# Transposing the first stage's tiles in pairs, and moving one evacuation of the second stage from ScalarE to VectorE

## The chip, the cores and the metric

The kernel runs on the 8 NeuronCores of one Trainium2 chip. Each core has a tensor engine (TensorE, PE in the profile), a vector engine (VectorE, DVE), a scalar engine (ScalarE, ACT), GpSimd (POOL) and SyncE (SP), and 16 DMA engines. Every core works on one batch element, alone: the cores exchange nothing. The metric is the device time of the slowest core in microseconds (us). TensorE's clock has two levels here, 2.4 GHz (a granted clock of 1.00 in the profile) and 1.2 GHz (0.50).

## The reference

Each core computes, for its 4096 tokens of width 1024, one layer with a linear "attention" and a feed-forward part. Cut to what is computed:

```python
qkv = einsum('btd,de->bte', layernorm(x), Wqkv) + bqkv      # 1024 -> 3072
q = q / norm(q); k = k / norm(k)
kv = sum(k * v, axis=tokens)                                 # one row of 1024
x = x + einsum('btd,de->bte', q * kv, Wout) + bout
h = layer_norm(x) @ ternary_quant(w1).T + b1                 # 1024 -> 4096
h = layer_norm(gelu(h))
out = x + h @ ternary_quant(w2).T + b2                       # 4096 -> 1024
```

`kv` is a sum over all tokens, so everything after it needs a first pass over all of them. The ternary quantization needs the mean of the absolute values of a whole weight matrix before its first element can be rounded.

## The kernel before, in words

The 4096 tokens are 32 tiles of 128. The program is written by hand for each engine: every engine has its own list of instructions, in order, and semaphores say what one waits for of another. Nothing is scheduled automatically, so an instruction that waits holds up all that stand behind it on its engine.

**Stage A (to 870 us)** makes q, k and v. For tile j, SyncE loads x into `xbufA` (L293), VectorE and ScalarE compute the layer norm, ScalarE writes the normalised tile `h1buf` to a scratch in HBM (L359), and SyncE reads it back transposed into `h1T` (`h1t_tile`, L273 to L286), with eight DMA transposes of 128 rows by 128 columns, one for each 128-column block. `h1T` holds two groups of four tiles. TensorE multiplies it by Wqkv (L591): six blocks e0 to e5 of 512 columns, eight products each, into a ring of four PSUM buffers `pqkv`. VectorE takes them out three tiles later than it normalises (`dvA_back(j - 3)`, L835), and ScalarE and VectorE make `qhat`, `khat` and the sum of k times v. Beside this runs the weight quantization: GpSimd loads 128 slabs of w1 and w2 into a ring of five buffers `wstg` (L545) and writes the quantized ones back (L534, L538); VectorE sums absolute values (L785) or adds two sign tiles (L793), ScalarE makes the signs (L420, L422). One round of stage A's loop over j is called an iteration here.

Then the quantized weights are read back transposed (`w1p`, `w2p`: L309, L315) and scaled (to about 1060 us).

**Stage B (from about 1060 us)** handles the tiles in 16 pairs p, j0 = 2p and j1 = 2p + 1. In a pair TensorE does, in this order: the output projection of tile j0 + 2 (`attn_mm`, L670); y1, the first feed-forward product, for both tiles (L731, 32 steps m of eight products, into two PSUM buffers that ScalarE empties with Gelu into `h4buf`, L496); the projection of tile j1 + 2; the transposition of tile j0 + 2's normalised `z1buf` as two rounds of four 128 by 128 products with the identity into the one PSUM buffer `pzT` (`zT_round`, L711), where round 1 waits until round 0 has been taken out (semaphore `bze`); then y2 of tile j0 and y2 of tile j1 (`y2_tile`). Each of the 32 steps of y2 is two products of 512 columns (L690), a one-column product that sums h (L696), and one that sums its square (L699). The squares come from VectorE (`dv_h4sq`, L1004) over a ring of four small tiles `h4sq`: TensorE's L699 of step m waits for square m, and VectorE's square m + 4 waits for that L699. After y2 of each tile VectorE computes statistics and the output (`dv_tail`, L1014 to L1054), then the front of a later tile (`dv_front`, L961 to L990); y2 of the next tile waits for `outbuf` (L1054), and its first L699 for the square behind that front. The last two rounds of `zT_round`, for tile j1 + 2, lie inside and behind y2 of j1.

The transposed tile goes from `pzT` to `z1T` in two halves of four casts: by ScalarE for tile j0 + 2 (`zT_evac_sc`, L443 to L451, called at L501), by VectorE for tile j1 + 2 (`zT_evac`, L1057 to L1065, called at L1082).

Of the kernel before, what the change touches and what calls it, by code (L numbers as in the profile page):

```python
# [11 lines left out]
AF = mybir.ActivationFunctionType  # L12
# [43 lines left out]
def build_program(T):  # L56
    NT = T // 128
    NG = NT // 4
# [17 lines left out]
    h1_d = nc.dram_tensor("h1scr", [T, D], BF16, kind="Internal").ap()  # L76
# [42 lines left out]
    ax = DSem(nc, es, "ax"); asq = S("asq"); avar = S("avar"); asd = S("asd")  # L119
    astat = S("astat"); ah1 = S("ah1")  # L120
    ah1w = DSem(nc, es, "ah1w"); ah1t = DSem(nc, es, "ah1t", nslots=4)
# [71 lines left out]
    z1T = sbB("z1T", [128, 2048], BF16, is_transpose_dest=True)  # L193
# [18 lines left out]
    pzT = psB.enter_context(nc.psum_tensor("pzT", [128, 512], F32))  # L212
# [56 lines left out]
    with es, esB, psB, nc.Block() as block:  # L269

        @block.sync
        def _(sy):
            def h1t_tile(jt):  # L273
                gt = jt // 4
                st = jt % 4
                sy.wait_ge(ah1w.h(jt % 2), 16 * (jt // 2 + 1))
                if jt >= 4:
                    sy.wait_ge(ah1t.h(jt % 4), 128 * (jt // 4))
                if gt >= 2 and st == 0:
                    sy.wait_ge(aqkv.h, 24 * (gt - 1))  # L280
                for c in range(8):
                    ah1t.inc(sy.dma_start(
                        out=h1T[:, (gt % 2) * 4096 + c * 512 + st * 128:
                                (gt % 2) * 4096 + c * 512 + (st + 1) * 128],
                        in_=h1_d[jt * 128:(jt + 1) * 128, c * 128:(c + 1) * 128],
                        transpose=True), jt)  # L286

            for g in range(NG):
                for s in range(4):
                    j = 4 * g + s  # L290
                    if j >= 2:
                        sy.wait_ge(ah1.h, j - 1)
                    ax.inc(sy.dma_start(  # L293
                        out=xbufA[:, (j % 2) * D:(j % 2 + 1) * D],
                        in_=x_d[j * 128:(j + 1) * 128, :]), j)
                    if j - 2 >= 0:
                        h1t_tile(j - 2)
            for jt in (4 * NG - 2, 4 * NG - 1):
                h1t_tile(jt)
            sy.wait_ge(ax.h(0), ax.totals()[0])  # L300
            sy.wait_ge(ax.h(1), ax.totals()[1])
            for sl in range(4):
                sy.wait_ge(ah1t.h(sl), ah1t.totals()[sl])
            bar.inc(sy.nop())
            sy.wait_ge(bar.h, 5)
            for sl in range(4):
                sy.wait_ge(dvw.h(sl), 16 * 8)
            for c in range(8):
                w1t.inc(sy.dma_start(out=w1p[:, c * H:(c + 1) * H],  # L309
                                     in_=wq1_d[:, c * 128:(c + 1) * 128],  # L310
                                     transpose=True), 16)
            for sl in range(4):
                sy.wait_ge(dvw.h(sl), 16 * 16)
            for r in range(32):
                w2t.inc(sy.dma_start(out=w2p[:, r * D:(r + 1) * D],  # L315
                                     in_=wq2_d[:, r * 128:(r + 1) * 128],
                                     transpose=True), 16)
            for j in range(NT):
                if j >= 1:
                    sy.wait_ge(batt.h, 2 * j)  # L320
                for c in range(8):
                    bqt.inc(sy.dma_start(
                        out=qT[:, c * 128:(c + 1) * 128],
                        in_=qh_d[j * 128:(j + 1) * 128, c * 128:(c + 1) * 128],
                        transpose=True), 16)
                if j >= 2:
                    sy.wait_ge(bsqx.h, j - 1)
                bx.inc(sy.dma_start(out=xbufB[:, (j % 2) * D:(j % 2 + 1) * D],
                                    in_=x_d[j * 128:(j + 1) * 128, :]), j)
            sy.wait_ge(bow.h, 16 * NT)  # L330

        @block.scalar
        def _(sc):
# [106 lines left out]
            sc.wait_ge(bar.h, 5)  # L440
            smld.inc(sc.dma_start(out=b2rowB, in_=b2_d), 16)

            def zT_evac_sc(t, r):  # L443
                g = 2 * t + r
                sc.wait_ge(bzt.h, g + 1)
                for cc in range(4):
                    c = 4 * r + cc
                    cp = sc.activation(
                        out=z1T[:, c * 256 + (t % 2) * 128:c * 256 + (t % 2) * 128 + 128],
                        in_=pzT[:, cc * 128:(cc + 1) * 128], func=AF.Copy)  # L450
                bze.inc(cp)  # L451

            def sc_front(t):
                P = (t % 2) * 16
                xr = xring[:, (t % 3) * D:(t % 3 + 1) * D]
# [32 lines left out]
            for p in range(NT // 2):  # L488
                j0, j1 = 2 * p, 2 * p + 1
                if j0 + 2 < NT:  # L490
                    sc_front(j0 + 2)
                if p >= 1:
                    sc.wait_ge(bsq4.h, 32 * j0)
                for m in range(32):
                    sc.wait_ge(by1.h, 32 * p + m + 1)
                    bh4.inc(sc.activation(  # L496
                        out=h4buf[:, m * 256:(m + 1) * 256],
                        in_=py1[m % 2][:, :], func=AF.Gelu,
                        bias=beta1c[:, m:m + 1]))
                if j0 + 2 < NT:  # L500
                    zT_evac_sc(j0 + 2, 0)  # L501
                    zT_evac_sc(j0 + 2, 1)
                sc_tail(j0)
                if j1 + 2 < NT:
                    sc_front(j1 + 2)
                sc_tail(j1)
# [61 lines left out]
        def _(te):  # L568
# [13 lines left out]
            te.wait_ge(wqkvs.h, 128)  # L582
            for g in range(NG):
                for s in range(4):
                    te.wait_ge(ah1t.h(s), 128 * (g + 1))
                    for e in range(6):
                        i = (4 * g + s) * 6 + e
                        if i >= 4:
                            te.wait_ge(aevac.h, i - 3)
                        for c in range(8):  # L590
                            mm = te.matmul(  # L591
                                out=pq[i % 4][:, :],
                                lhsT=h1T[:, (g % 2) * 4096 + c * 512 + s * 128:
                                         (g % 2) * 4096 + c * 512 + (s + 1) * 128],
                                rhs=wqkvp[:, c * E3 + e * 512:c * E3 + (e + 1) * 512],
                                start=(c == 0), stop=(c == 7))
                        aqkv.inc(mm)
                    if (g, s) == p_mtot1:
                        te.wait_ge(mpre.h, 1)
                        mtot.inc(te.matmul(out=pone[:, 0:1],  # L600
                                           lhsT=stA[:, 30:31], rhs=onesf[:, :],
                                           start=True, stop=True))
                    if (g, s) == p_mbc1:
                        te.wait_ge(mval.h, 1)
                        mbc.inc(te.matmul(out=pmb[:, 0:1], lhsT=onesrow[:, :],
                                          rhs=mrow[0:1, 0:1],
                                          start=True, stop=True))
                    if (g, s) == p_mtot2:
                        te.wait_ge(mpre.h, 2)
                        mtot.inc(te.matmul(out=pone[:, 1:2],  # L610
                                           lhsT=stA[:, 31:32], rhs=onesf[:, :],
                                           start=True, stop=True))
                    if (g, s) == p_mbc2:
                        te.wait_ge(mval.h, 2)
                        mbc.inc(te.matmul(out=pmb[:, 1:2], lhsT=onesrow[:, :],
                                          rhs=mrow[0:1, 1:2],
                                          start=True, stop=True))
# [103 lines left out]
            for p in range(NT // 2):  # L721
                j0, j1 = 2 * p, 2 * p + 1
# [4 lines left out]
                for m in range(32):  # L727
                    if 32 * p + m >= 2:
                        te.wait_ge(bh4.h, 32 * p + m - 1)
                    for c in range(8):  # L730
                        mm = te.matmul(  # L731
                            out=py1[m % 2][:, :],
# [15 lines left out]
        def _(dv):  # L748
# [323 lines left out]
            for p in range(NT // 2):  # L1072
                j0, j1 = 2 * p, 2 * p + 1
                if j0 + 2 < NT:
                    dv_front(j0 + 2)
                dv_h4sq(j0)
                dv_tail(j0)
                if j1 + 2 < NT:
                    dv_front(j1 + 2)
                dv_h4sq(j1)  # L1080
                if j1 + 2 < NT:
                    zT_evac(j1 + 2, 0)  # L1082
                    zT_evac(j1 + 2, 1)
                dv_tail(j1)
# [17 lines left out]
        "bfin": NT, "bow": 16 * NT,  # L1102
        "bzt": 2 * NT, "bze": 2 * NT,
    }
    dexpect = {"ax": 16 * NT, "ah1w": 16 * NT, "ah1t": 512 * NG,
               "aqw": 16 * NT, "wld": 16 * NLOADS,
               "dvw": 16 * (NW1 + NW2),
               "bx": 16 * NT}
# [43 lines left out]
```

## Time and profile before

| what | value |
|---|---|
| three runs | 2606.44, 2609.64, 2615.18 us; median 2609.64 |
| the profiled execution | 2606.68 us, its slowest core's span 2605.1 us |
| spans of the eight cores | 2581.4 to 2605.1 us |
| mean granted TensorE clock | 0.814 to 0.824 |
| busy: PE, DVE, ACT, POOL | 62%, 38%, 31%, 5% of the span |
| chain of work that ended last, by engine | PE 49%, DVE 12%, issue 9%, ACT 9%, DVEq 8%, DMA 7% |
| the same by line, the largest | y2 L690 19%, y1 L731 18%, qkv L591 7%, wstg loads 5% |
| landing time of an h1T transpose (SP, 256 of them) | 2.8 us |

The page cuts the span into 40 slices of 65 us. Stage A is slices 2 to 14; from slice 17 on PE's row repeats 867 867 867, which are the pairs of stage B. The page's shares are averages over both stages, so what follows is read from the trace in the stretch where each edit acts. Busy times and rows below are of the slowest core, core 0.

### The profile page before, as it was taken

How to read it: one execution, taken by the hardware profiler on the slowest of the kernel's cores; microseconds unless marked ns; L12 is line 12 of the kernel's file. 1: busy time of each engine (PE TensorE's matmuls, PEld its weight loads, DVE VectorE, ACT ScalarE, POOL GpSimd, SP SyncE). 2: the span in 40 equal slices, each digit the busy share in tenths (PEclk: the TensorE clock that was granted, in tenths of full speed). 3: DMA queues.
4: the chain of work that ended last, by engine and by line, in shares of the span. 5: the costliest groups of instructions: out<-in, count | busy, mean ns of one | idle time of the engine just before them, and what ended most of it. 6: DMA issues, size and time to landing. Idle time of an engine off the chain costs nothing.

```text
span 2605.1 us, 35302 instructions; the slowest of 8 cores (2581.4 to 2605.1 us)
## 1 busy us (share of the span) xinstructions
PE 1624.3 (62%) x10800; PEld 911.5 (35%) x10928; DVE 989.7 (38%) x2582; ACT 795.0 (31%) x1433; POOL 118.5 (5%) x217
## 2 busy tenths in 40 slices
PE   0354565453457226767867867867867867867867
PEld 0121222121123112435535535535535534534544
DVE  0456644443445223252252252252252252252243
ACT  0132356656664100313313313313313312312311
POOL 2111101111110000000000000000000000000000
PEclk9976777677778657878888888888888888888889
DMA  9776544555542590110010010010010010010000
GB/s 146 177 212 200 162 122 145 174 168 161 176 150 69 117 152 14 34 41 21 21 41 22 21 42 21 22 41 22 22 40 21 22 40 22 23 40 21 21 17 17
DMA packets 203594, 195.39 MB, mean 75 GB/s; under 512 B 160404, under 2 KB 160405, under 8 KB 203415
## 3 DMA queue, kind: packets, MB, share of 16 engines
q0 software_dynamic: 31200, 92.34, 12.9%
q1 hardware_dynamic: 157952, 67.18, 11.1%
q10 hardware_dynamic: 14264, 33.62, 3.6%
q8 instruction: 97, 1.59, 0.3%
q14 instruction: 81, 0.66, 0.1%
HBM read 117.55 MB, written 50.33 MB: 64 GB/s over the span
## 4 chain that ended last, share of the span: by engine, by line
PE 49%; DVE 12%; issue 9%; ACT 9%; DVEq 8%; DMA 7%; SPq 4%; POOL 1%; ACTq 1%; another core or an unknown queue 0%; POOLq 0%
PE py L690 19%; PE py L731 18%; PE pqkv L591 7%; DMA wstg<-w 5%; PE patt L670 3%; DVEq L962 2%; DVEq L805 2%; SPq L315 2%; SPq L309 2%; DVE outbuf L1046 2%; DVEq L1053 1%; DVE kvtmp L846 1%; DVE xring L967 1%; ACT qhat L379 1%; ACT khat L388 1%
## 5 line engine op out<-in xcount | busy, mean ns | idle before, releaser
L591 PE MATMUL pqkv<-wqkvp,h1T 128*128 128x512 bf16 x1505 | 402.3, 432 | 366.8 <-DVE qkvb L835 334.2
L690 PE MATMUL py<-w2p,h4buf 128*128 128x512 bf16 x1968 | 528.6, 398 | 134.5 <-DVE outbuf L1054 123.1
L731 PE MATMUL py<-z1T,w1p 128*128 128x256 bf16 x4096 | 491.3, 285 | 167.3 <-ACT h4buf L496 165.5
L1004 DVE TENSOR_TENSOR h4sq<-h4buf 128x128 bf16<-128x128 bf16 x1024 | 227.3, 225 | 847.9 <-PE psumSQ L699 711.1
L731 PEld LDWEIGHTS py<-z1T,w1p 128*128 128x128 bf16 x4096 | 388.9, 101 | 270.4 <-issue 172.5
L591 PEld LDWEIGHTS pqkv<-wqkvp,h1T 128*128 128x128 bf16 x1536 | 163.7, 108 | 604.9 <-issue 470.7
L496 ACT ACTIVATE h4buf<-py,beta1c 128x256 bf16<-128x256 f32 x512 | 241.1, 474 | 239.4 <-PE py L731 238.7
L699 PE MATMUL psumSQ<-onesb,h4sq 128*128 128x1 bf16 x1024 | 167.4, 163 | 76.3 <-DVE h4sq L1004 76.3
L699 PEld LDWEIGHTS psumSQ<-onesb,h4sq 128*128 128x128 bf16 x1024 | 102.7, 100 | 215.5 <-issue 104.7
L696 PE MATMUL psumSQ<-onesb,h4buf 128*128 128x1 bf16 x1024 | 173.3, 169 | 0.0
L690 PEld LDWEIGHTS py<-w2p,h4buf 128*128 128x128 bf16 x2048 | 125.5, 96 | 127.7 <-issue 127.3
L835 DVE TENSOR_TENSOR qkvb<-pqkv,bqkvb 128x512 f32<-128x512 f32 x192 | 123.7, 686 | 110.5 <-PE pqkv L591 103.6
L696 PEld LDWEIGHTS psumSQ<-onesb,h4buf 128*128 128x128 bf16 x1024 | 103.3, 101 | 138.5 <-issue 28.3
L458 ACT ACTIVATE xbufB<-xring 128x512 f32<-128x512 f32 x32 | 20.1, 629 | 402.7 <-DVE xring L967 402.7
L670 PE MATMUL patt<-woutp,qT 128*128 128x512 bf16 x495 | 118.1, 393 | 14.5 <-DMA qT<-qhscr 13.2
L480 ACT ACTIVATE stB<-stB 128x1 f32<-128x1 f32 x32 | 6.5, 203 | 308.9 <-DVE stB L1031 308.7
L480 ACT ACT_TABLE_LOAD x16 | 20.5, 1283 | 257.7 <-DVE stB L1031 257.7
L785 DVE TENSOR_REDUCE wpart<-wstg 128x1 f32<-128x1024 f32 x64 | 74.4, 1213 | 17.9 <-DMA wstg<-w 17.9
L349 ACT ACTIVATE stA<-stA 128x1 f32<-128x1 f32 x32 | 6.5, 203 | 243.7 <-DVE stA L816 243.7
L545 POOL DMA_DIRECT2D wstg<-w x128 | 68.0, 532 | 234.2 <-DVE wpart L785 233.4
L846 DVE TENSOR_TENSOR kvtmp<-khat,qkvb 128x1024 f32<-128x1024 f32 x32 | 39.2, 1226 | 98.9 <-ACT khat L388 98.9
L670 PEld LDWEIGHTS patt<-woutp,qT 128*128 128x128 bf16 x512 | 50.8, 101 | 73.3 <-issue 23.8
(126 smaller groups left out, 1275.6 us busy)
## 6 DMA issues: line engine op xcount, KB each, us to landing
wstg<-w POOLq DMA_DIRECT2D x128, 512.0 KB, 5.9
xbufA<-x SPq DMA_DIRECT2D x32, 512.0 KB, 5.0
xbufB<-x SPq DMA_DIRECT2D x32, 512.0 KB, 3.5
out<-outbuf ACTq DMA_DIRECT2D x32, 512.0 KB, 2.7
h1scr<-h1buf ACTq DMA_DIRECT2D x32, 256.0 KB, 5.1
qhscr<-qhat ACTq DMA_DIRECT2D x32, 256.0 KB, 2.4
wqkvp<-wqkv POOLq DMA_DIRECT2D x8, 768.0 KB, 28.8
h1T<-h1scr SPq DMA_TRANSPOSE x256, 2.8
```

Of the source, the lines that this page charges most:

```text
L496: bh4.inc(sc.activation(out=h4buf[:, m * 256:(m + 1) * 256], in_=py1[m % 2][:, :], func=AF.Gelu, bias=beta1c[:, m:m + 1]))
L545: wld.inc(gp.dma_start(out=wslot(i), in_=w_src(kind, ch)), i)
L591: mm = te.matmul(out=pq[i % 4][:, :], lhsT=h1T[:, (g % 2) * 4096 + c * 512 + s * 128: (g % 2) * 4096 + c * 512 + (s + 1) * 128], rhs=wqkvp ...
L670: mm = te.matmul(out=patt[:, hh * 512:(hh + 1) * 512], lhsT=qT[:, c * 128:(c + 1) * 128], rhs=woutp[:, c * D + hh * 512:c * D + (hh + 1) * ...
L690: mm = te.matmul(out=py2[:, hh * 512:(hh + 1) * 512], lhsT=h4m, rhs=w2p[:, m * D + hh * 512:m * D + (hh + 1) * 512], start=(m == 0), stop= ...
L696: te.matmul(out=psumSQ[:, m:m + 1], lhsT=h4m, rhs=onesb[:, :], start=True, stop=True)
L699: bsq4.inc(te.matmul(out=psumSQ[:, 32 + m:33 + m], lhsT=h4sq[:, (m % 4) * 128:(m % 4 + 1) * 128], rhs=onesb[:, :], start=True, stop=True))
L731: mm = te.matmul(out=py1[m % 2][:, :], lhsT=w1p[:, c * H + m * 128:c * H + (m + 1) * 128], rhs=z1T[:, c * 256:(c + 1) * 256], start=(c == ...
L785: dcons.inc(dv.tensor_reduce(out=wpart[:, col:col + 1], in_=wslot(i), axis=AX.X, op=ALU.add, apply_absolute_value=True))
L835: aevac.inc(dv.tensor_tensor(out=qkvb[:, e * 512:(e + 1) * 512], in0=pq[i % 4][:, :], in1=bqkvb[:, e * 512:(e + 1) * 512], op=ALU.add))
L846: dv.tensor_tensor(out=kvtmp[:, :], in0=khat[:, :], in1=qkvb[:, 2 * D:3 * D], op=ALU.mult)
L1004: bsq.inc(dv.tensor_tensor(out=h4sq[:, (m % 4) * 128:(m % 4 + 1) * 128], in0=h4m, in1=h4m, op=ALU.mult))
```

## The change: pairs of tiles in stage A, one evacuation in stage B

Two edits that do not touch each other.

In stage A `h1t_tile` becomes `h1t_half`: it transposes two tiles in one go, so each of its eight DMA transposes reads 256 rows and writes 256 columns of `h1T`. It is called once for every two tiles, after the x load of tile jt + 3, and waits until both tiles have been written to HBM. The semaphores `ah1t` count pairs.

In stage B `zT_evac_sc` is gone; VectorE calls `zT_evac(j0 + 2, 0)` and `zT_evac(j0 + 2, 1)` between the front of tile j0 + 2 and the squares of tile j0.

```diff
--- before.py
+++ after.py
@@ -270,20 +270,22 @@
 
         @block.sync
         def _(sy):
-            def h1t_tile(jt):
+            def h1t_half(jt):
                 gt = jt // 4
                 st = jt % 4
-                sy.wait_ge(ah1w.h(jt % 2), 16 * (jt // 2 + 1))
-                if jt >= 4:
-                    sy.wait_ge(ah1t.h(jt % 4), 128 * (jt // 4))
+                hg = jt // 2
+                sy.wait_ge(ah1w.h(0), 16 * (jt // 2 + 1))
+                sy.wait_ge(ah1w.h(1), 16 * (jt // 2 + 1))
+                if hg >= 4:
+                    sy.wait_ge(ah1t.h(hg % 4), 128 * (hg // 4))
                 if gt >= 2 and st == 0:
                     sy.wait_ge(aqkv.h, 24 * (gt - 1))
                 for c in range(8):
                     ah1t.inc(sy.dma_start(
                         out=h1T[:, (gt % 2) * 4096 + c * 512 + st * 128:
-                                (gt % 2) * 4096 + c * 512 + (st + 1) * 128],
-                        in_=h1_d[jt * 128:(jt + 1) * 128, c * 128:(c + 1) * 128],
-                        transpose=True), jt)
+                                (gt % 2) * 4096 + c * 512 + (st + 2) * 128],
+                        in_=h1_d[jt * 128:(jt + 2) * 128, c * 128:(c + 1) * 128],
+                        transpose=True), hg)
 
             for g in range(NG):
                 for s in range(4):
@@ -293,10 +295,9 @@
                     ax.inc(sy.dma_start(
                         out=xbufA[:, (j % 2) * D:(j % 2 + 1) * D],
                         in_=x_d[j * 128:(j + 1) * 128, :]), j)
-                    if j - 2 >= 0:
-                        h1t_tile(j - 2)
-            for jt in (4 * NG - 2, 4 * NG - 1):
-                h1t_tile(jt)
+                    if j >= 3 and j % 2 == 1:
+                        h1t_half(j - 3)
+            h1t_half(4 * NG - 2)
             sy.wait_ge(ax.h(0), ax.totals()[0])
             sy.wait_ge(ax.h(1), ax.totals()[1])
             for sl in range(4):
@@ -440,16 +441,6 @@
             sc.wait_ge(bar.h, 5)
             smld.inc(sc.dma_start(out=b2rowB, in_=b2_d), 16)
 
-            def zT_evac_sc(t, r):
-                g = 2 * t + r
-                sc.wait_ge(bzt.h, g + 1)
-                for cc in range(4):
-                    c = 4 * r + cc
-                    cp = sc.activation(
-                        out=z1T[:, c * 256 + (t % 2) * 128:c * 256 + (t % 2) * 128 + 128],
-                        in_=pzT[:, cc * 128:(cc + 1) * 128], func=AF.Copy)
-                bze.inc(cp)
-
             def sc_front(t):
                 P = (t % 2) * 16
                 xr = xring[:, (t % 3) * D:(t % 3 + 1) * D]
@@ -497,9 +488,6 @@
                         out=h4buf[:, m * 256:(m + 1) * 256],
                         in_=py1[m % 2][:, :], func=AF.Gelu,
                         bias=beta1c[:, m:m + 1]))
-                if j0 + 2 < NT:
-                    zT_evac_sc(j0 + 2, 0)
-                    zT_evac_sc(j0 + 2, 1)
                 sc_tail(j0)
                 if j1 + 2 < NT:
                     sc_front(j1 + 2)
@@ -582,7 +570,8 @@
             te.wait_ge(wqkvs.h, 128)
             for g in range(NG):
                 for s in range(4):
-                    te.wait_ge(ah1t.h(s), 128 * (g + 1))
+                    hg = 2 * g + s // 2
+                    te.wait_ge(ah1t.h(hg % 4), 128 * (hg // 4 + 1))
                     for e in range(6):
                         i = (4 * g + s) * 6 + e
                         if i >= 4:
@@ -1073,6 +1062,8 @@
                 j0, j1 = 2 * p, 2 * p + 1
                 if j0 + 2 < NT:
                     dv_front(j0 + 2)
+                    zT_evac(j0 + 2, 0)
+                    zT_evac(j0 + 2, 1)
                 dv_h4sq(j0)
                 dv_tail(j0)
                 if j1 + 2 < NT:
@@ -1102,7 +1093,7 @@
         "bfin": NT, "bow": 16 * NT,
         "bzt": 2 * NT, "bze": 2 * NT,
     }
-    dexpect = {"ax": 16 * NT, "ah1w": 16 * NT, "ah1t": 512 * NG,
+    dexpect = {"ax": 16 * NT, "ah1w": 16 * NT, "ah1t": 64 * NT,
                "aqw": 16 * NT, "wld": 16 * NLOADS,
                "dvw": 16 * (NW1 + NW2),
                "bx": 16 * NT}
```

VectorE in the first pair of stage B. Before, the squares of j0 (`h4sq`) follow the front's last statistic directly; `bzt` is TensorE's transposition being done, `bh4` ScalarE's Gelu, `bsq4` TensorE's L699:

```order
L988 RECIPROCAL stB<-stB 128x1 [waits bsd]
L990 TENSOR_TENSOR stB<-stB 128x1
L1004 TENSOR_TENSOR h4sq<-h4buf 128x128 [waits bh4] x4
L1004 TENSOR_TENSOR h4sq<-h4buf 128x128 [waits bh4,bsq4] x28
L1014 TENSOR_REDUCE stB<-psumSQ 128x1 [waits bsq4]
```

The same place now:

```order
L977 RECIPROCAL stB<-stB 128x1 [waits bsd]
L979 TENSOR_TENSOR stB<-stB 128x1
L1051 CAST z1T<-pzT 128x128 [waits bzt]
L1051 CAST z1T<-pzT 128x128 x3
L1051 CAST z1T<-pzT 128x128 [waits bzt]
L1051 CAST z1T<-pzT 128x128 x3
L993 TENSOR_TENSOR h4sq<-h4buf 128x128 [waits bh4] x4
L993 TENSOR_TENSOR h4sq<-h4buf 128x128 [waits bh4,bsq4] x28
L1003 TENSOR_REDUCE stB<-psumSQ 128x1 [waits bsq4]
```

All 32 squares of tile j0 now stand behind eight casts that wait for TensorE's transposition; before, the first four waited for Gelu alone.

SyncE in stage A, from its first x loads on. `ah1` is ScalarE's normalised tile, `ah1w0` and `ah1w1` its write to HBM for even and odd tiles. Before:

```order
L293 DMA xbufA<-x 128x1024 x2
L293 DMA xbufA<-x 128x1024 [waits ah1]
L282 DMA_TRANSPOSE h1T<-h1scr 128x128 [waits ah1w0]
L282 DMA_TRANSPOSE h1T<-h1scr 128x128 x7
L293 DMA xbufA<-x 128x1024 [waits ah1]
L282 DMA_TRANSPOSE h1T<-h1scr 128x128 [waits ah1w1]
L282 DMA_TRANSPOSE h1T<-h1scr 128x128 x7
```

And now:

```order
L295 DMA xbufA<-x 128x1024 x2
L295 DMA xbufA<-x 128x1024 [waits ah1] x2
L284 DMA_TRANSPOSE h1T<-h1scr 128x256 [waits ah1w0,ah1w1]
L284 DMA_TRANSPOSE h1T<-h1scr 128x256 x7
L295 DMA xbufA<-x 128x1024 [waits ah1] x2
L284 DMA_TRANSPOSE h1T<-h1scr 128x256 [waits ah1w0,ah1w1]
L284 DMA_TRANSPOSE h1T<-h1scr 128x256 x7
```

Two x loads now stand ahead of each batch of eight transposes, and the batch waits for the write of the later tile of its pair.

## Rows read from the trace of the kernel before

**Rows 1.** Waits in 1300 to 2605 us: total us, times, longest us.

```profile
PE py L731 <- ACT h4buf L496: 136.8, 13, 11.2
...
PE py L690 <- DVE outbuf L1054: 107.5, 14, 7.7
```

**Rows 2.** Timeline of PE, stage A: start, length, instruction, [idle before, releaser].

```profile
119.47 9.70 PE L591 MATMUL pqkv<-wqkvp,h1T 128*128 128x512 bf16 x32 [30.03 <-DMA h1T<-h1scr]
...
495.07 6.18 PE L591 MATMUL pqkv<-wqkvp,h1T 128*128 128x512 bf16 x16 [14.21 <-DVE qkvb L835]
...
834.05 10.52 PE L591 MATMUL pqkv<-wqkvp,h1T 128*128 128x512 bf16 x47 [0.37 <-DVE qkvb L835]
```

**Rows 3.** The chain that ended last, stage A: start, length, what.

```profile
139.63 4.32 PE pqkv L591 x14
...
509.49 4.16 DMA wstg<-w
...
591.42 5.68 DMA wstg<-w
```

**Rows 4.** Timeline of SyncE's queue.

```profile
99.61 12.01 SPq L282 DMA_TRANSPOSE h1T<-h1scr  x8
...
114.08 11.20 SPq L282 DMA_TRANSPOSE h1T<-h1scr  x8
...
473.91 10.03 SPq L282 DMA_TRANSPOSE h1T<-h1scr  x8
...
500.12 10.04 SPq L282 DMA_TRANSPOSE h1T<-h1scr  x8
...
578.78 10.02 SPq L282 DMA_TRANSPOSE h1T<-h1scr  x8
...
796.80 40.00 SPq L282 DMA_TRANSPOSE h1T<-h1scr  x24
...
915.92 53.81 SPq L315 DMA_TRANSPOSE w2p<-wq2scr  x32
```

**Rows 5.** Timeline of DVE in stage A, first tile taken out.

```profile
137.99 2.48 DVE L835 TENSOR_TENSOR qkvb<-pqkv,bqkvb 128x512 f32<-128x512 f32 x4
```

**Rows 6.** Timeline of PE around the transposition in one pair.

```profile
1398.16 0.39 PE L711 MATMUL pzT<-identb,z1buf 128*128 128x128 bf16 x4
1399.85 0.38 PE L711 MATMUL pzT<-identb,z1buf 128*128 128x128 bf16 x4 [1.31 <-ACT z1T L448]
...
1400.75 0.16 PE L699 MATMUL psumSQ<-onesb,h4sq 128*128 128x1 bf16 x1
...
1429.59 0.16 PE L699 MATMUL psumSQ<-onesb,h4sq 128*128 128x1 bf16 x1 [5.04 <-DVE h4sq L1004]
```

**Rows 7.** Timeline of ACT at the same place.

```profile
1400.33 0.79 ACT L448 ACTIVATE z1T<-pzT 128x128 bf16<-128x128 f32 x4 [0.62 <-PE pzT L711]
```

**Rows 8.** Timeline of DVE in the same pair.

```profile
1370.69 0.23 DVE L1004 TENSOR_TENSOR h4sq<-h4buf 128x128 bf16<-128x128 bf16 x1 [1.48 <-ACT h4buf L496]
...
1429.22 0.93 DVE L1004 TENSOR_TENSOR h4sq<-h4buf 128x128 bf16<-128x128 bf16 x5
...
1448.10 0.88 DVE L1062 CAST z1T<-pzT 128x128 bf16<-128x128 f32 x4 [1.27 <-PE pzT L711]
1448.90 0.18 DVE L1014 TENSOR_REDUCE stB<-psumSQ 128x1 f32<-128x32 f32 x1
```

**Rows 9.** Windows: length, busy us of PE, PEld, DVE, ACT, POOL, PEclk, DMA share, GB/s.

```profile
1333.10:1339.10 6.00, 5.66 (x36) 2.66 (x37) 2.34 (x12) 0.93 (x1) 0.00 (x0) 0.71 0.00 0
1429.59:1435.59 6.00, 5.66 (x26) 2.39 (x28) 1.87 (x10) 0.94 (x1) 0.00 (x0) 0.50 0.00 1
1366.37:1372.37 6.00, 6.00 (x36) 4.53 (x37) 0.90 (x4) 1.80 (x5) 0.00 (x0) 0.64 0.12 49
1464.02:1470.02 6.00, 6.00 (x30) 4.21 (x31) 0.90 (x4) 1.65 (x4) 0.00 (x0) 0.53 0.13 51
...
1269.37:2436.74 1167.37, 860.83 (x6649) 536.25 (x6722) 415.74 (x1344) 309.09 (x697) 0.00 (x0) 0.86 0.09 28
```

## The prediction, made before the changed kernel had run

> **What bounds the kernel now.** I read the cores' spans, the chain that ended last, and then for each edit the waits and the timelines of the stretch in which it acts. In stage B the chain runs through TensorE, so what counts is where TensorE stands still. The waits and the timeline show three such places in a pair [rows 1]: before y1's third step for ScalarE's first Gelu (about 10.8 us, behind the output and the front of a tile), before y2 of j1 for `outbuf` (7.7 us), and a little later for j1's first square. None of them is touched. A fourth, small, wait lies between the two transposition rounds. After it TensorE goes straight into y2 of j0, because four squares were made long before.
>
> In stage A TensorE is not the bound: it waits 14.2 us for VectorE [rows 2] in an iteration of some 26 us. The chain there goes round through VectorE, TensorE's last 16 products of a tile, ScalarE, VectorE, GpSimd and one weight load of 4.2 to 5.7 us [rows 3]. SyncE's transposes are not in it; they take 10 of the 26.2 us from one batch to the next [rows 4].
>
> **Edit 1: transposes in pairs.** The same bytes move in 128 DMAs instead of 256.
>
> *Cost on SyncE.* Eight transposes of 128 rows are issued in 10.03 us, 1.25 us each; the weight transposes of 1024 rows in 53.81 / 32 = 1.68 us each [rows 4]. Between these, 256 rows should take 1.25 + (0.43 / 896) x 128 = 1.31 us, so a pair's batch takes 10.5 us. Bounds: 10.0 (price by the instruction) and 20.1 us (price by the row). Per two iterations SyncE is busy 10.5 us instead of 20; it was idle over half of the time, so that frees nothing.
>
> *The middle of stage A.* The pair's batch starts when the later tile's write has landed, 5.05 us after TensorE has resumed in that iteration (495.07 and 500.12 [rows 2, 4]), and with the 2.8 us that the profile's table gives for a landing it is there after 5.05 + 10.5 + 2.8 = 18.4 us. TensorE wants the earlier tile one iteration later, behind the last 16 products of the tile before (6.18 us [rows 2]): 26.2 + 6.2 = 32.4 us. Slack 14 us; with the high bound of the batch still 4 us. The two tiles of a group reuse a half of `h1T` that was free long before. Taken: nothing. What hides it is VectorE's hold on TensorE.
>
> The Trainium skill, "DMA: Bandwidth & Descriptors", section "Anatomy of one DMA", gives each DMA a constant part of about 2 us, mostly completion. If that were on the path, 128 DMAs fewer would be worth an estimated 256 us, and the sum would be near 2380 us. The trace speaks against applying it: the issues follow each other 1.25 us apart, so these parts overlap, and nobody waits for them after the first tile. The sum goes by the rows.
>
> *The start.* TensorE's first tile waits for the first batch. Now this batch waits for tile 1 too, so it starts where tile 1's batch started, 114.08, and is issued by 125.3 [rows 4]. The first batch before (99.61 + 12.01 = 111.62 [rows 4]) was followed by TensorE at 119.47 [rows 2], 7.9 us later, which gives 133.2 us; with the usual landing of 2.8 us it is 128.1. TensorE's first 32 products take 9.70 us, so they end between 137.8 and 142.9. VectorE has them out by 137.99 + 2.48 = 140.5 now [rows 5]; TensorE's last 16 overlap that, since they may start when the first buffer is free (4.32 us for 14 from 139.63 [rows 3]). Delay 0 to 4 us; taken 2, the middle.
>
> *The end.* The last 24 transposes end at 796.80 + 40.00 = 836.80 [rows 4], so tile 31's batch began at 826.8. Tile 30 now goes with it: 826.8 + 10.5 + 2.8 = 840.1. TensorE reached tile 30 at 834.05 + 16 x 0.224 (10.52 us for 47 products) = 837.6 [rows 2]. Late by 2.5 us on a stretch where TensorE follows VectorE with 0.4 us of idle; taken 2, ends 0 and 12 (a batch of 20 us).
>
> Edit 1 together: +4 us; from -5 (transposes absent from every second iteration give the weight loads a little room) to +16.
>
> **Edit 2: the casts of tile j0 + 2 on VectorE.** There are 15 pairs with it. ScalarE loses eight casts, 1.58 us; behind them it only waits for VectorE's statistic at the end of y2 of j0, so nothing is gained there.
>
> *Round 0.* Four casts take 0.79 us on ScalarE [rows 7] and 0.88 us on VectorE [rows 8]; TensorE's round 1 waits for them: +0.09 us.
>
> *Round 1.* Now nobody waits for ScalarE's casts, and y2 follows. The squares m = 0 to 3 were done at 1370.9 [rows 8], thirty microseconds ahead, so the first L699 ran at 1400.75 [rows 6]. Afterwards VectorE waits from the end of its front until round 0. Queued behind the casts are all squares of j0, and behind these the output and the next front; TensorE waits for the first square. Round 1 ends at 1400.23, casts start at 1400.33 [rows 6, 7], take 0.88 us, and the next VectorE instruction starts 0.08 us before their nominal end, as 1448.90 after 1448.10 + 0.88 shows [rows 8]: 1401.13. From a first square's start to TensorE's L699 takes 1429.59 - 1429.22 = 0.37 us [rows 6, 8]: 1401.50. That is 0.75 us later than 1400.75. Squares then come every 0.18 us (five in 0.93) against TensorE's step of 0.48, so no second wait. Sum 0.84 us a pair, 15 x 0.84 = 12.6 us. Bounds: 0.6 us (if the square is seen at once) and 1.1 us (each semaphore wait of the new chain adding about 0.1).
>
> *What the clock makes of it.* After both long waits of a pair the clock is at 1.2 GHz when work resumes, and stays there for some microseconds. In windows of 6 us from the resumption it is 0.71 and 0.50 of full after the first wait, in one pair and the next, 0.64 and 0.53 after the second [rows 9]. The part at 1.2 GHz is thus 3.5 or 6.0 us and 4.3 or 5.7 us, and half of it is lost work: 3.9 us in the short kind of pair, 5.8 us in the long kind. The two kinds alternate along the whole stage, and twelve pairs take 1167.37 us, 97.28 each. So the pairs run in step with the clock's changes, two by two, with a mean loss of 4.85 us. Each pair longer by 0.84 us breaks this step. In the short kind the clock rose barely after 3.5 us of resumed work; if work resumes 0.8 us later against that rise, the rise falls to the later occasion, as in the long kind. I expect nearly all pairs to be of the long kind: loss 5.7 instead of 4.85, +0.86 us. A pair then takes 97.28 + 0.84 + 0.86 = 98.98 us. Bounds: all short, -0.96; all long, +0.96. I take a value near the upper end, since a delay can only move the resumption away from the early rise. 15 x 1.70 = 25.5 us.
>
> **The sum.** 25.5 + 4 = 29.5 us on the profiled execution's 2606.68: 2636 us. Its span was 2605.1, the rest is start and end. The median of the three runs is 3 us above it; the same would hold for the changed kernel: 2639 us.
>
> **The rivals.**
>
> *A, only the added wait counts.* The alternation stays as it is, by chance of the new phase, and a pair costs 0.84 us: 12.6 + 4 = 16.6, so 2626 us. For it: the added wait is the only thing in the listing. Against it: the exact alternation shows that the pair's length and the clock hang together.
>
> *B, the other side: the weight loads get faster.* In iterations without transposes the load on stage A's chain could take 4.16 us, the shortest of its late ones, instead of 5.68. If that held for all 26 iterations from tile 4 to 29, it would give 26 x 1.52 = 40 us, and the time would be 2599 us, faster. It decides from a saving of 1.1 us an iteration on. For it: halved DMAs and 10 us of idle queue. Against it: the load at 591.42, behind transposes that had all been issued by 588.8, still took 5.68 us, and the one of 4.16 us began before its transposes (500.1 to 510.2) were over [rows 3, 4]. So the length does not follow the transposes.
>
> *C, the clock falls at the transposition.* TensorE would be idle 1.4 us and again 0.8 us with half a microsecond of work between, where now it is idle once and the clock stays at 1.00. If it fell there, y2 would run its first steps at 1.2 GHz and lose what the resumption after the first wait loses in the long kind, 3.0 us: 15 x 3.0 = 45 more, 2684 us. The Trainium skill, "TensorE: Matmul & The Clock Gate", section "A second HAM failure mode: psum-queue depth-cycling", says that short idle spells between groups of matmuls can be enough to make the clock swing. By that rule the time would be this rival's. The trace does not bear it out so far: the idle 1.31 us here leaves the clock up [rows 6], and y2's steps run on at 0.48 us.
>
> **How the numbers follow.** Forecast 0.62, A 0.22, B 0.06, C 0.04, and 0.06 for a mixture of B with A, in which both edits cancel. The likeliest gives 2639 us. Its own range is 2628 to 2650 (the rhythm between 0.4 and 0.96 a pair, edit 1 between -2 and +12). The range downwards takes in A with edit 1 at -5 (2617). Upwards it takes the high ends of the wait (+4) and of edit 1: 2653. A change within 0.3% (8 us) can't be told from none. Slower by more: forecast, most of A, and C, 0.88; faster, B, 0.06; same 0.06.
>
> **What would show it.** Right: in each of 15 pairs an idle stretch of 0.7 to 0.8 us before the first L699 of j0, put down to VectorE's square; VectorE's casts there at 0.88 us, ScalarE without casts; y2 of j0 still at 0.48 us a step; pairs of 98.9 to 99.1 us on average with a mean clock in stage B no higher than 0.86; 128 transposes in stage A, eight in 10 to 11 us. TensorE's first product at 128 to 133 us. Wrong: pairs that still average under 98.3 us (rival A), iterations of stage A clearly shorter than 26 us (B), a clock of 0.50 in the stretch after round 1 (C), or TensorE waiting for `h1T` in the middle of stage A, which would mean that a batch takes far longer than 11 us.

## The result, and the profile after

The changed kernel is slower: the median of ten runs is 2642.6 us against 2608.8 us of ten runs of the kernel before, a ratio of 1.0125, 95% interval 1.0111 to 1.0139. The forecast was 2639 us. Some executions fall into a slower state of the chip, so every ratio here is of the undisturbed runs alone, while the medians are of all runs.

The profiled execution took 2641.46 us with a span of 2639.9 us on core 0, the core whose rows stood before. First stage A, PE's timeline after:

```profile
142.55 19.18 PE L580 MATMUL pqkv<-wqkvp,h1T 128*128 128x512 bf16 x79 [52.64 <-DMA h1T<-h1scr]
...
840.01 11.52 PE L580 MATMUL pqkv<-wqkvp,h1T 128*128 128x512 bf16 x47 [3.57 <-DVE qkvb L824]
851.89 10.52 PE L580 MATMUL pqkv<-wqkvp,h1T 128*128 128x512 bf16 x47 [0.36 <-DVE qkvb L824]
```

TensorE gets its first tile 23.1 us later than in [rows 2] (142.55 against 119.47; 128 to 133 had been forecast), and that is the only wait for `h1T` in the whole run: at the end of stage A its idle times are put down to VectorE, as before. VectorE, which takes the first tile out:

```profile
133.91 0.16 DVE L812 TENSOR_TENSOR stA<-stA 128x1 f32<-128x1 f32 x1
146.23 0.69 DVE L824 TENSOR_TENSOR qkvb<-pqkv,bqkvb 128x512 f32<-128x512 f32 x1 [12.16 <-PE pqkv L580]
```

It is ready 4 us earlier than in [rows 5] and then stands for 12.2 us; the first buffer goes out 8.2 us later than before. The batches of transposes, SyncE's queue:

```profile
115.82 13.24 SPq L284 DMA_TRANSPOSE h1T<-h1scr  x8
...
488.37 10.13 SPq L284 DMA_TRANSPOSE h1T<-h1scr  x8
```

Eight transposes of 256 rows are issued in 10.1 us, as fast as eight of 128 rows [rows 4]. The first batch took 13.2 us and landed 13.5 us after its last issue (115.82 + 13.24 = 129.06, TensorE at 142.55), where the first batch before landed after 7.9 us. In these 13.5 us the core's DMA engines are busy all the time (a mean share of 1.01), while beside the batch at 488.37 their share is 0.44:

```profile
129.10:142.50 13.40, 0.00 (x0) 0.00 (x0) 3.25 (x9) 1.44 (x2) 1.06 (x2) 1.00 1.01 232
488.30:502.00 13.70, 6.65 (x31) 2.83 (x29) 5.16 (x8) 9.09 (x8) 3.21 (x6) 0.84 0.44 128
```

The first batch before met full DMA engines too (shares 1.05 and 0.98), with half the bytes. That the load makes the landing so long fits, but no run varies it alone.

Now stage B, in one pair. PE and then DVE around the transposition:

```profile
1412.56 0.39 PE L700 MATMUL pzT<-identb,z1buf 128*128 128x128 bf16 x4
1414.08 0.38 PE L700 MATMUL pzT<-identb,z1buf 128*128 128x128 bf16 x4 [1.14 <-DVE z1T L1051]
1414.53 0.59 PE L679 MATMUL py<-w2p,h4buf 128*128 128x512 bf16 x2
1414.95 0.17 PE L685 MATMUL psumSQ<-onesb,h4buf 128*128 128x1 bf16 x1
1415.74 0.16 PE L688 MATMUL psumSQ<-onesb,h4sq 128*128 128x1 bf16 x1 [0.62 <-DVE h4sq L993]
```

```profile
1414.57 0.89 DVE L1051 CAST z1T<-pzT 128x128 bf16<-128x128 f32 x4 [0.64 <-PE pzT L700]
1415.37 0.86 DVE L993 TENSOR_TENSOR h4sq<-h4buf 128x128 bf16<-128x128 bf16 x5
```

The chain casts, first square, first L699 (L688 now) is there as foretold. From y2's first product to that L699 it takes 1.21 us where it took 0.46 (1400.29 to 1400.75, [rows 6] for the latter): 0.75 us more, 0.73 on the mean of the 15 pairs. From round 0 to round 1 it is 1.52 us in all pairs after and 1.41 in 14 of 15 before, 0.09 us more on the mean; only the pair of [rows 6] had 1.69. Together the two waits add 0.82 us a pair. The clock's windows after, one pair and the next after the first long wait (y2 of j1 for its first square), one pair and the next after the second (y1 for the Gelu), then the beginning of y2 of j0, and twelve pairs:

```profile
1347.30:1353.30 6.00, 5.66 (x34) 2.68 (x36) 2.21 (x12) 0.93 (x1) 0.00 (x0) 0.69 0.00 1
1446.65:1452.65 6.00, 5.66 (x37) 2.70 (x39) 2.35 (x12) 0.93 (x1) 0.00 (x0) 0.72 0.00 0
1380.70:1386.70 6.00, 6.00 (x36) 4.38 (x37) 0.00 (x0) 1.72 (x5) 0.00 (x0) 0.63 0.16 63
1480.15:1486.15 6.00, 6.00 (x38) 4.47 (x39) 0.00 (x0) 1.95 (x5) 0.00 (x0) 0.67 0.08 33
1415.90:1419.30 3.40, 3.40 (x14) 1.29 (x15) 0.99 (x5) 0.00 (x0) 0.00 (x0) 0.50 0.13 28
1281.65:2469.59 1187.94, 872.86 (x6649) 538.26 (x6722) 432.55 (x1440) 289.80 (x601) 0.00 (x0) 0.86 0.09 28
```

A pair takes 1187.94 / 12 = 99.00 us, 1.71 more than in [rows 9]; 98.98 had been forecast. But it comes about in another way. Nearly all pairs are now of the short kind after both long waits. Measured from where work resumes to where the granted clock rises, on the mean of these twelve pairs of core 0, the low stretch after the first wait was 4.65 us before and is 3.85 now, the one after the second was 4.89 and is 4.49. In exchange the clock is at 1.2 GHz for 3.4 us at the start of y2 of j0, where it was 1.00 before:

```profile
1398.50:1401.90 3.40, 2.03 (x18) 1.09 (x18) 0.45 (x2) 1.57 (x8) 0.00 (x0) 1.00 0.10 22
```

It falls so in 12 of the 15 pairs on core 0, and in 12 or 13 on every core. In the other three pairs of core 0 the clock stays up, with a second idle spell of 0.47, 0.47 and 0.83 us where the twelve have 0.53 to 0.62; the low stretches after the long waits that follow are then longer.

### The profile page after: what moved, and what is told of

The parts are those of the page before. It is cut to its first block, busy times and chain, and to the rows that moved or that the text cites. A ratio compares the mean times of both kernels' runs of the same rounds, so it can differ in the third digit from the quotient of the medians.

```text
span 2639.9 us, 35158 instructions; the slowest of 8 cores (2610.9 to 2639.9 us)
## 1 busy us (share of the span) xinstructions
PE 1629.5 (62%) x10800; PEld 911.8 (35%) x10928; DVE 1010.8 (38%) x2702; ACT 771.0 (29%) x1313; POOL 118.0 (4%) x217
## 4 chain that ended last, share of the span: by engine, by line
PE 49%; DVE 13%; issue 9%; ACT 8%; DVEq 7%; DMA 7%; SPq 5%; POOL 1%; ACTq 1%; another core or an unknown queue 0%; POOLq 0%
PE py L679 19%; PE py L720 17%; PE pqkv L580 7%; DMA wstg<-w 5%; PE patt L659 2%; DVEq L951 2%; DVEq L794 2%; SPq L316 2%; SPq L310 2%; DVE outbuf L1035 2%; DVEq L1042 1%; DVE kvtmp L835 1%; DVE xring L956 1%; ACT qhat L380 1%; ACT khat L389 1%
## 5 line engine op out<-in xcount | busy, mean ns | idle before, releaser
L679 PE MATMUL py<-w2p,h4buf 128*128 128x512 bf16 x1968 | 543.6, 405 | 135.6 <-DVE outbuf L1043 124.1
L1051 DVE CAST z1T<-pzT 128x128 bf16<-128x128 f32 x256 | 56.6, 283 | 567.9 <-PE pzT L700 567.3
L688 PE MATMUL psumSQ<-onesb,h4sq 128*128 128x1 bf16 x1024 | 167.5, 164 | 84.5 <-DVE h4sq L993 84.5
L688 PEld LDWEIGHTS psumSQ<-onesb,h4sq 128*128 128x128 bf16 x1024 | 104.2, 102 | 231.1 <-issue 125.9
```

The lines of the kernel that those rows point to most:

```text
L679: mm = te.matmul(out=py2[:, hh * 512:(hh + 1) * 512], lhsT=h4m, rhs=w2p[:, m * D + hh * 512:m * D + (hh + 1) * 512], start=(m == 0), stop= ...
L688: bsq4.inc(te.matmul(out=psumSQ[:, 32 + m:33 + m], lhsT=h4sq[:, (m % 4) * 128:(m % 4 + 1) * 128], rhs=onesb[:, :], start=True, stop=True))
```

## The experiments

All ran in two groups of four, each group on one chip with its own runs of the kernel before (medians 2599.6 and 2599.5 us; these chips are 9 us faster than the one of the result, so ratios are compared, not times). The traces allow a comparison by stage as well, on the mean of the eight cores: when the sum over tokens starts at the end of stage A, and the time from TensorE's first product of y1 to the end.

| kernel | chip | sum over tokens starts, us | first y1 product to the end, us |
|---|---|---|---|
| before | of the result | 861.3 | 1539.2 |
| the change | of the result | 869.2 | 1564.1 |
| edit 1 alone | first group | 864.6 | 1538.7 |
| edit 2 alone | first group | 859.3 | 1564.0 |
| four squares first | first group | 859.4 | 1539.5 |
| four products | first group | 855.4 | 1563.8 |
| twelve products | second group | 855.5 | 1564.5 |
| first two tiles singly | second group | 856.8 | 1539.2 |
| four squares of j1 ahead | second group | 858.0 | 1474.6 |
| seven squares, earlier release | second group | 855.4 | 1460.2 |

Each line is one profile. Kernels with the same stage A on the same chip differ by up to 4 us in the first column; kernels with the same stage B agree within 1 us in the second.

**Edit 1 alone.** The change without its stage B part (ScalarE's casts put back).

> Edit 1 alone: stage A transposes in pairs, stage B as before. The changed kernel's TensorE got its first tile at 142.6 us instead of 119.5. Theory S (the late start is passed on and is edit 1's whole cost): 8 to 13 us slower than before, 2618 to 2622, TensorE's first product of stage A again near 142, pairs of stage B 97.4 to 97.5 us. Rival (stage A swallows the late start, as slack or by faster weight loads): within 3 us of before. Rival B (faster iterations): faster than before.

Measured: 2604.1 us, ratio 1.0029 (1.0018 to 1.0041). PE's first product of stage A and one of the last, core 0:

```profile
140.05 19.58 PE L593 MATMUL pqkv<-wqkvp,h1T 128*128 128x512 bf16 x80 [53.34 <-DMA h1T<-h1scr]
...
872.10 3.55 PE L623 MATMUL pkv<-onesf,kv_acc 128*128 128x1 f32 x16 [6.77 <-DVE kv_acc L851]
```

The late first tile is there; the time is 7.5 us longer by the ratio, just under what theory S gave and far above no change. The fair comparison is with the three kernels of this group that have stage A as before. Against their mean the fifth tile is normalised 10.0 us later (167.9 against 157.9 us), and the sum over tokens starts 6.6 us later (864.6 against 858.0 us). So later iterations give some 3 us back, which is no more than the other three profiles differ among themselves. Stage B takes what it took before (1538.7 against 1539.2 us).

**The first two tiles singly, all others in pairs** (again without edit 2):

```
-   if j >= 3 and j % 2 == 1: h1t_half(j - 3)
+   if j in (2, 3):           h1t_one(j - 2)        # 8 x [128,128], as before
+   elif j >= 3 and j % 2 == 1: h1t_half(j - 3)
```

> Edit 1 alone, but tiles 0 and 1 transposed singly as before (batches of eight 128x128), all later tiles in pairs. Theory (edit 1's cost is the late first tile): TensorE's first product near 119 us again, the fifth tile normalised near 160 us, and 4 to 8 us faster than edit 1 alone, so 0 to 4 us faster than before, since the run with edit 1 alone made good some 5 us later in stage A. Rival (pairs cost in the middle or at the end): as edit 1 alone, 0.3% slower than before.

Measured: 2601.3 us, ratio 1.0010 (0.9986 to 1.0034).

```profile
117.83 9.33 PE L610 MATMUL pqkv<-wqkvp,h1T 128*128 128x512 bf16 x32 [29.25 <-DMA h1T<-h1scr]
```

TensorE starts at 118 us again and the fifth tile is normalised at 158.5 us (mean of eight cores). The sum over tokens starts at 856.8 us, against 856.3 us on the mean of the other three kernels of this group: no gain from pairs elsewhere shows. By the times it cannot be said, since the interval reaches from -4 to +9 us. TensorE has no long wait for `h1T` after the start in either kernel. That the late first tile causes most of edit 1's cost is shown by the traces; by the times it is only likely, since the two intervals overlap.

**Edit 2 alone.** Before, with `zT_evac` for tile j0 + 2 on VectorE as in the change.

> Edit 2 alone: the casts of tile j0 + 2 on VectorE, stage A as before. Theory (stage B's loss is all of this edit): pairs 99.0 to 99.1 us as in the changed kernel instead of 97.46, 15 x 1.6 = 24 us slower than before, 2633, and the clock at 1.2 GHz for some microseconds at the beginning of y2 of j0 in most pairs. Additive rival: 0.84 us a pair, 13 us, 2622.

Measured: 2622.8 us, ratio 1.0091 (1.0075 to 1.0108), +24 us. Eleven pairs and two looks at the start of y2 of j0, core 0:

```profile
1285.40:1288.60 3.20, 3.20 (x14) 1.24 (x15) 0.96 (x5) 0.00 (x0) 0.00 (x0) 0.50 0.12 26
1384.40:1387.60 3.20, 3.20 (x14) 1.22 (x13) 0.93 (x5) 0.00 (x0) 0.00 (x0) 0.50 0.10 21
...
1349.14:2438.00 1088.86, 807.50 (x6160) 493.88 (x6161) 396.53 (x1320) 265.61 (x551) 0.00 (x0) 0.86 0.09 28
```

98.99 us a pair with the clock's fall, and 1564.0 us from the first y1 product to the end against the 1564.1 of the whole change: stage B's loss is all of this edit, and the additive rival (13 us) is out. With edit 1's 0.29% the two make 1.20%, the whole change 1.25%.

**The same with four squares first.** The casts stay on VectorE, but behind the first four squares of j0:

```
-   zT_evac(j0 + 2, 0); zT_evac(j0 + 2, 1); dv_h4sq(j0)
+   dv_h4sq(j0, 0, 4); zT_evac(j0 + 2, 0); zT_evac(j0 + 2, 1); dv_h4sq(j0, 4, 32)
```

> Edit 2 with the first four squares of j0 ahead of VectorE's eight casts, stage A as before. Theory (the cost is TensorE's wait for the first square and what follows of it, not the casts on VectorE): no wait at the first L699, clock at 1.00 there, pairs 97.4 to 97.6 us, 0 to 3 us slower than before. Rival (casts on VectorE cost by themselves, by their 0.88 us or by the squares queued behind them): pairs 98 us or more, 10 us or more slower.

Measured: 2601.0 us, ratio 0.9996 (0.9977 to 1.0015). PE at the same place, core 0:

```profile
1388.78 0.38 PE L698 MATMUL pzT<-identb,z1buf 128*128 128x128 bf16 x4 [1.14 <-DVE z1T L1049]
1389.22 0.59 PE L677 MATMUL py<-w2p,h4buf 128*128 128x512 bf16 x2
1389.65 0.17 PE L683 MATMUL psumSQ<-onesb,h4buf 128*128 128x1 bf16 x1
1389.68 0.16 PE L686 MATMUL psumSQ<-onesb,h4sq 128*128 128x1 bf16 x1
```

The first L699 follows 0.46 us behind y2's first product, without a wait. All 24 us of edit 2 are gone though VectorE does the same casts, so they hung on the order alone. The clock falls at this place in no pair, although the first idle spell is as long as in the change (1.14 us).

**The wait's length as work.** Before, with four more products ahead of y2 of j0, their result overwritten by y2's first step; then with twelve:

```
+   if j % 2 == 0 and j + 2 < NT:
+       for _ in range(4):       # 12 in the other kernel
+           te.matmul(out=py2[:, 0:512], lhsT=identb, rhs=woutp[:, 0:512], ...)
```

> Before, with four more products of 128x512 on TensorE (0.86 us at 2.4 GHz, result overwritten) ahead of y2 of j0 in 15 pairs: the added wait's length, but as work, so that the clock has no idle stretch to fall in. Additive theory: 0.86 us a pair, pairs 98.3 us, 13 us slower, 2622. Rhythm theory (the pair's length settles against the clock, whatever makes it longer): pairs 98.9 to 99.0 us, 22 to 25 us slower, 2632, with the longer kind of low-clock stretch after both long waits. Theory that only the clock's fall at the new idle place costs the rest: as the additive one.

> Before, with twelve more products of 128x512 (2.6 us at 2.4 GHz, result overwritten) ahead of y2 of j0 in 15 pairs, three times the work that was added in the run with four. Additive theory: a pair 2.6 us longer than 97.46, or 1.7 us longer than with four products: pairs 99.8 to 100.1, 37 to 40 us slower than before. Rhythm theory (pairs settle at certain lengths; the four products were already charged 1.5 us, and the rest of that step is free): pairs 99.0 to 99.2 us, 25 to 28 us slower, hardly more than with four.

Measured: with four 2624.0 us, ratio 1.0102 (1.0080 to 1.0124), +26 us; with twelve 2627.3 us, ratio 1.0111 (1.0093 to 1.0130), +29 us. The clock after the first long wait in two pairs, after the second in two pairs, then eleven pairs; first with four products (core 0), then with twelve (core 1):

```profile
1293.86:1299.86 6.00, 6.00 (x27) 2.40 (x28) 1.87 (x10) 0.93 (x1) 0.00 (x0) 0.51 0.00 0
1392.89:1398.89 6.00, 6.00 (x27) 2.42 (x28) 1.87 (x10) 0.94 (x1) 0.00 (x0) 0.51 0.01 1
1328.28:1334.28 6.00, 6.00 (x30) 4.35 (x31) 0.90 (x4) 1.64 (x4) 0.00 (x0) 0.53 0.14 57
1427.29:1433.29 6.00, 6.00 (x31) 4.36 (x32) 0.90 (x4) 1.64 (x4) 0.00 (x0) 0.53 0.10 40
...
1328.28:2417.06 1088.78, 816.14 (x6204) 500.23 (x6205) 380.96 (x1232) 282.88 (x639) 0.00 (x0) 0.84 0.09 28
```

```profile
1330.37:1336.37 6.00, 6.00 (x35) 2.63 (x36) 2.27 (x12) 0.93 (x1) 0.00 (x0) 0.70 0.00 0
1429.60:1435.60 6.00, 6.00 (x38) 2.72 (x39) 2.35 (x12) 0.94 (x1) 0.00 (x0) 0.72 0.00 1
1363.71:1369.71 6.00, 6.00 (x36) 4.40 (x37) 0.90 (x4) 1.77 (x5) 0.00 (x0) 0.63 0.12 48
1462.81:1468.81 6.00, 6.00 (x37) 4.51 (x38) 0.90 (x4) 1.83 (x5) 0.00 (x0) 0.64 0.09 38
...
1363.71:2452.42 1088.71, 816.00 (x6292) 500.91 (x6293) 380.52 (x1232) 283.78 (x639) 0.00 (x0) 0.88 0.09 28
```

98.98 and 98.97 us a pair. 0.86 us of work lengthened a pair by 1.7 us, and another 1.73 us of work by nothing at all. With four products every pair is of the long kind, with twelve every pair is of the short kind: the work that was added went where low-clock time had been. On the means of eleven pairs the low stretches after the first and the second long wait are 5.9 and 5.6 us with four products, 3.5 and 4.3 us with twelve. The additive theory (+13 and +37 to 40 us) is out in both runs. So is the theory that only the clock's fall at the transposition makes the wait dear: with four products the clock does not fall there, and the pair is as long. Why the pairs prefer this length is not shown by any run.

**The other direction.** If an added 0.8 us costs double, a saved wait could bring more than itself. Before, with the first four squares of j1 made in tile j0's tail while VectorE waits for ScalarE's square root:

```
     bvar2.inc(...)
+    if ahead is not None: dv_h4sq(ahead, 0, 4)
     dv.wait_ge(bsd2.h, j + 1)
```

> Before, with VectorE's first four squares of j1 moved into tile j0's tail, where VectorE waits for ScalarE's square root. Nothing is left out. TensorE can then do four steps of y2 of j1 (1.93 us at 2.4 GHz) in the gap where it waited 5.0 us for the first square. Additive theory: 1.9 us less a pair, pairs 95.5 us, 16 pairs, 30 us faster. Rhythm theory: pairs settle at 95.5 to 95.6 us, 25 to 30 us faster. Here the two agree. Theory that this wait is not what ends last there (the front is): no change.

Measured: 2536.8 us, ratio 0.9761 (0.9745 to 0.9778), 62 us faster, double of what both theories gave. PE at the start of y2 of j1 in one pair, core 0, with the rows of the first and the fifth step, and then the window of twelve pairs:

```profile
1385.59 1.01 PE L690 MATMUL py<-w2p,h4buf 128*128 128x512 bf16 x2 [7.67 <-DVE outbuf L1056]
...
1389.21 1.01 PE L690 MATMUL py<-w2p,h4buf 128*128 128x512 bf16 x2
...
1391.58 0.16 PE L699 MATMUL psumSQ<-onesb,h4sq 128*128 128x1 bf16 x1 [1.35 <-DVE h4sq L1004]
...
1391.70 0.59 PE L690 MATMUL py<-w2p,h4buf 128*128 128x512 bf16 x2
...
1392.16 0.16 PE L699 MATMUL psumSQ<-onesb,h4sq 128*128 128x1 bf16 x1
```

```profile
1234.02:2349.51 1115.49, 852.03 (x6649) 531.57 (x6722) 413.29 (x1344) 308.62 (x697) 0.00 (x0) 0.89 0.09 29
```

The products of the first steps run in the gap with 1.01 us for two of them, at 1.2 GHz; then TensorE waits 1.35 us for the fifth square, and when it comes the steps follow each other in 0.48 us (1391.70 to 1392.16 and on), at the full clock:

```profile
1391.58:1397.58 6.00, 5.92 (x49) 3.10 (x51) 3.18 (x15) 1.00 (x1) 0.00 (x0) 1.00 0.00 1
```

A pair takes 1115.49 / 12 = 92.96 us where it took 97.28 [rows 9], 4.3 us less. Four steps of 0.48 us are 1.9 us of that. The rest is low clock that TensorE no longer works through. After this wait it resumed at 1.2 GHz for 4.65 us on the mean of twelve pairs; now the clock is up at once in nine pairs and low for 3.4 us in three, 0.85 us on the mean. Half of the difference is 1.9 us. After the other long wait the low stretch is 3.7 us instead of 4.9, another 0.6 us. The sum is 4.4 us, against 4.3 measured. The expectation had counted only the first part. These pairs have no common length: nine take 92.0 to 92.6 us, three 95.0 to 95.3.

**The same further.** A ring of seven squares, seven of them made ahead, and y2's wait for `py2` released after L1046 has read it instead of after L1054.

> Before, with seven squares of j1 in tile j0's tail, a ring of seven squares instead of four, and y2's wait for py2 released when VectorE has read py2 (L1046) instead of when the output is finished (L1054). Nothing is left out. TensorE starts y2 of j1 2.5 us earlier and has seven steps (3.4 us at 2.4 GHz) to do before the front of the next tile is over. Additive theory: 3.4 us less a pair, pairs 94.1 us, 53 us faster. Rhythm theory: pairs at 93.8 to 94.0, 50 to 55 us faster. Rival (the longer squares block delays VectorE's tail and front): pairs 95 us or more.

Measured: 2532.4 us, ratio 0.9719 (0.9682 to 0.9757), 73 us faster where 50 to 55 had been expected. PE's waits at the start of y2 of j1, core 0:

```profile
1383.76 1.01 PE L690 MATMUL py<-w2p,h4buf 128*128 128x512 bf16 x2 [5.18 <-DVE outbuf L1048]
...
1392.59 0.16 PE L699 MATMUL psumSQ<-onesb,h4sq 128*128 128x1 bf16 x1 [2.64 <-DVE h4sq L1004]
```

TensorE starts 2.5 us earlier (idle 5.18 instead of 7.67 us), and after seven steps stands 2.64 us for the eighth square, where the run with four stood 1.35 us: most of the head start is spent waiting for the front on VectorE. By the ratios the further step is not shown to be faster, since the two intervals just overlap; of the four runs behind its ratio three took 2518.6 to 2520.0 us and one 2544.8. The traces do put it ahead, 1460.2 against 1474.6 us from the first y1 product to the end. Either version is over 2% faster than the kernel before, and so than the changed kernel too.

## Why the prediction was right, point by point

- *The place and size of the new wait* (edit 2, rounds 0 and 1): right. 0.73 us before the first L699 where 0.75 had been computed, 0.09 us more between the rounds.
- *"I expect nearly all pairs to be of the long kind"*: this step was wrong, although its number, +0.86 us a pair, was nearly right. After the long waits the lost work fell, from (4.65 + 4.89) / 2 = 4.8 to (3.85 + 4.49) / 2 = 4.2 us a pair. The clock fell at the transposition instead, 3.4 us long in ten of the twelve pairs, which is 1.4 us of lost work a pair. So 0.82 - 0.6 + 1.4 = 1.6 us, against 1.7 measured. That +0.86 from one place and +0.8 from another agree so well is luck as far as the place goes.
- *What would show it*: of the signs named, the pairs of 99.0 us, the mean clock of 0.86, VectorE's casts at 0.88 us and the issue of the transposes came true. Three did not: TensorE's first product came at 142.6 us and not by 133, the first four steps of y2 of j0 took 0.8 to 1.0 us each instead of 0.48, and the clock of 0.50 behind round 1 was named as the sign of rival C.
- *Rival C*, with 0.04, described that fall. It happened, at 1.7 us and not 3.0 a time, and not on top of the forecast as C had it. The rule of the Trainium skill, "TensorE: Matmul & The Clock Gate", section "A second HAM failure mode: psum-queue depth-cycling", was right that the clock would fall here (0.50 for 3.4 us); the 2684 us worked out for it were not. I had set it aside because one idle spell of 1.3 us had left the clock up.
- *That the pair's length and the clock hang together*: right. Pairs of 99.0 us came out with the fall (edit 2), with long low stretches (four products) and with short ones (twelve). Which of the three it is made no difference to the pair's length. What sets that length is open.
- *Rival A* (0.84 us a pair): out, by edit 2 alone and by four products.
- *Rival B* (faster weight loads): out; edit 1 alone is slower.
- *The estimate of 256 us for 128 DMAs fewer*, made from the Trainium skill's "DMA: Bandwidth & Descriptors", section "Anatomy of one DMA": rightly left out of the sum. Edit 1 alone, with 128 DMAs fewer, took 1.0029 of the time before. The section describes DMAs issued by GpSimd; these are issued by SyncE.
- *The middle of stage A*: right, no wait for `h1T`. The batch took 10.1 us, which is the low bound (price by the instruction) rather than the 10.5 taken.
- *The start*, 0 to 4 us, taken 2: mis-sized. The batch landed 13.5 us after its last issue, not 2.8 to 7.9, VectorE got the first buffer 8.2 us late, and the fifth tile was normalised 10 us late. This is the term of the sum that was mis-sized. The bound had been taken from a batch of half the bytes.
- *The end*, taken 2: no wait for `h1T` there. Edit 1 in sum: 4 taken, 7.5 (4.7 to 10.7) measured.
- *The sum*: 25.5 + 4 forecast; 24 + 7.5 measured with the edits alone, 33 together. Edit 1 cost 3.5 us more than taken, edit 2 1.5 us less; the measured median is 3.6 us above the forecast.

## What to carry to other kernels

An instruction stream that waits for something late must not stand ahead of work that is ready and that somebody else will need: four squares made before the casts were worth 24 us. When a loop goes round with idle gaps long enough to drop TensorE's clock, measure the loop's whole length on the chip, since the added wait alone (0.82 us) gave half of the cost (1.7 us); and look for work to put into such a gap, since here it also took most of the slow restart with it. A transfer on a start-up path may be worth splitting small, even if in the steady state the large one costs no more: the first two tiles singly brought the start back.

## What the runs showed of the hardware

- Pairs of stage B averaged 97.3 us before, and 98.97 to 99.00 us in four kernels with 0.8 to 2.6 us more in the pair, whether spent waiting or working.
- TensorE's clock fell to 1.2 GHz at a place where idle spells of 1.1 and 0.6 us stood close together; it did so in 12 or 13 of 15 pairs. With the first alone (1.14 us, four squares first; 1.0 to 1.3 us before) it stayed at 2.4 GHz in all of them.
- A DMA transpose of 256 rows by 128 columns was issued in the same time as one of 128 rows (eight in 10.1 and in 10.0 us). Its median landing was 3.1 us against 2.8 us.
- A first batch of eight such transposes landed 13.5 us after its last issue while the DMA engines were fully busy, one of eight 128-row transposes 7.9 us.
